# Routing stage of a fused four-layer kernel: three parties of expert places, all shared-expert steps in one stage

## The reference

```
logits = flat @ router_w                       # 2048 x 64 experts
_, topk_idx = top_k(logits + router_bias, 4)   # 4 experts for each token
comb = softmax scores of those 4, made to sum to 1
g = silu(flat @ wg[e]);  u = flat @ wu[e]
routed = sum over e of comb * ((g * u) @ wd[e])
shared = sum over s of (silu(flat @ swg[s]) * (flat @ swu[s])) @ swd[s]
out = routed + shared
```

## Time and profile before

| | us |
|---|---|
| runs shown | 1292.83, 1293.5, 1296.53 (median 1293.5) |
| profiled execution | 1294.35, with a span of 1292.6 |
| busy: TensorE, VectorE, ScalarE, GpSimd | 1117.1, 867.2, 615.2, 407.7 |
| routing stage | 234 to 357.4, the experts' first load at 361.5 |
| stage behind the experts | first gather at 497.3, last at 596.3 |

### The profile page before, as it was taken

One profiled execution on the slowest core, in us unless ns is written; L12 is line 12 of the kernel. 1 busy time (PEld: TensorE's weight loads), 2 busy tenths in 40 slices (PEclk: granted clock), 3 DMA queues, 4 the chain that ended last, 5 costly groups with the idle time before them and its releaser, 6 DMA issues. The chain is left out here.

```text
span 1292.6 us, 31608 instructions
## 1 busy us (share of the span) xinstructions
PE 1117.1 (86%) x12162; PEld 916.7 (71%) x12162; DVE 867.2 (67%) x2172; ACT 615.2 (48%) x1404; POOL 407.7 (32%) x592
## 2 busy tenths in 40 slices
PE   5569998547689997777779999999999999999987
PEld 4446776445478996665547888888888888888776
DVE  5467997757646766688556667666766686664565
ACT  4434455222234443466735554555455555553654
POOL 3331122067700455784038005400530152000221
PEclk9879999757889998888789999999999999999999
DMA  6747785222289884354233334233352342232001
GB/s 161 182 125 203 215 230 185 98 74 90 93 330 417 292 280 164 104 177 143 87 108 110 94 95 143 85 85 105 124 156 85 112 118 91 84 103 84 1 17 50
DMA packets 78562, 177.74 MB, mean 138 GB/s; under 512 B 12678, under 2 KB 26246, under 8 KB 75846
## 3 DMA queue, kind: packets, MB, share of 16 engines
q1 hardware_dynamic: 72140, 158.67, 38.6%
q0 software_dynamic: 6272, 17.05, 4.4%
HBM read 114.40 MB, written 61.08 MB: 136 GB/s over the span
## 5 line engine op out<-in xcount | busy, mean ns | idle before, releaser
L2318 ACT ACTIVATE decay<-masked,negcum 128x128 f32<-128x128 f32 x512 | 163.1, 391 | 102.8 <-DVE mixT L2382 102.8
L2226 PE MATMUL joint<-xh,w_high 128*128 128x512 f32 x512 | 209.3, 409 | 2.0 <-POOL wl L2162 2.0
L2226 PE MATMUL joint<-xl,w_high 128*128 128x512 f32 x512 | 200.2, 391 | 0.0
L2226 PE MATMUL joint<-xh,wl 128*128 128x512 f32 x512 | 199.9, 390 | 0.0
L2430 DVE COPY cT<-joint 128x512 f32<-128x512 f32 x128 | 88.3, 690 | 86.0 <-PE joint L2226 85.7
L2336 ACT ACTIVATE bT<-joint 128x512 f32<-128x512 f32 x128 | 76.6, 599 | 129.9 <-PE joint L2226 129.9
L2382 DVE TENSOR_TENSOR mixT<-pcb,decay 128x512 f32<-128x512 f32 x128 | 82.4, 685 | 57.8 <-PE pcb L2242 57.8
L2159 POOL TENSOR_TENSOR w_high<-w_in,none 128x512 fp32r<-128x512 f32 x32 | 37.0, 1155 | 260.4 <-DMA w_in<-in_w_bc 250.0
L2226 PEld LDWEIGHTS joint<-xh,w_high 128*128 128x128 f32 x512 | 96.2, 188 | 23.6 <-POOL wl L2162 2.4
L2226 PEld LDWEIGHTS joint<-xh,wl 128*128 128x128 f32 x512 | 96.1, 188 | 20.8
L2226 PEld LDWEIGHTS joint<-xl,w_high 128*128 128x128 f32 x512 | 96.3, 188 | 17.0
(11 more groups left out here) (373 smaller groups left out, 2715.7 us busy)
## 6 DMA issues: line engine op xcount, KB each, us to landing
cumrow<-ssm_cum SPq DMA_DIRECT2D x128, 256.0 KB, 3.3
slots_in<-blank SPq DMA_DIRECT2D x16, 1024.0 KB, 5.6
rows<-slots_in SPq DMA_DIRECT2D x32, 512.0 KB, 5.1
slots_out<-spare SPq DMA_DIRECT2D x32, 512.0 KB, 3.8
weights<-in_expert_quads SPq DMA_DIRECT2D x16, 768.0 KB, 9.1
w_in<-in_w_bc SPq DMA_DIRECT2D x32, 256.0 KB, 3.7
qk_parts<-parts SPq DMA_DIRECT2D x32, 192.0 KB, 2.3
stack<-qk_parts SPq DMA_DIRECT2D x32, 192.0 KB, 5.4
```

Of the source, the lines that this page charges most:

```text
L2226: last = nc.tensor.matmul(bank[:], w[:, j, col:col + P], a[:, k, c * CHUNK:(c + 1) * CHUNK], start=(m == 0), stop=(m == len(parts) - 1))
L2318: last = nc.scalar.activation(decay[:, n % 2, o], masked[:, n % 2, o], ACT.Exp, bias=negcum[:, c * TPC + i, head:head + 1])
```

## The change

Expert places are given out in three parties of 1, 1 and 2 chunks (`PARTY`); counts and ranks are summed by party. All 16 shared steps run in the routing stage: steps 0 to 3 (chunk 0) ahead of chunk 2's transposes, the other twelve behind `place_chunk(3)`. On VectorE a step is cut into `product` and `low`, which are spread between other work, one `low` even inside `find_slots`. The deviations of x of chunks 2 and 3 stand ahead of scatters 12 and 16. In the stage behind the experts the splits, the late steps, their loads and their copies are gone, and `first` is (0, 2, 2, 0).

```diff
-PARTIES = 2
+PARTY = [0, 1, 2, 2]
+PARTIES = PARTY[-1] + 1
-BEFORE_ROWS = 6
-LATE = 2
-NOW = NCH - LATE
+BEFORE_ROWS = {12: 2, 16: 3}
...
-    STEPS = SHARED * NOW
+    STEPS = SHARED * NCH
...
-                            if n == BEFORE_ROWS:
-                                for late in range(EARLY_NORMS, NCH):
-                                    deviations(OF_X, late)
+                            if n in BEFORE_ROWS:
+                                deviations(OF_X, BEFORE_ROWS[n])
...
                 turn(0)
                 turn(1)
                 score(0)
-                score(1)
                 place_chunk(0)
+                score(1)
+                pe.wait_ge(logits_out, 1)
+                up(0)
                 place_chunk(1)
-                turn(2)
-                score(2)
-                turn(3)
-                score(3)
+                pe.wait_ge(logits_out, EARLY_NORMS)
+                for n in range(1, SHARED):
+                    up(n)
+                    down(n - 1)
+                down(SHARED - 1)
+                pe.wait_ge(y_out, 1)
+                turn(2)
+                turn(3)
+                score(2)
+                score(3)
                 place_chunk(2)
                 place_chunk(3)
                 pe.wait_ge(logits_out, NCH)
...
+                for n in range(SHARED, STEPS):
+                    up(n)
+                    if n > SHARED:
+                        down(n - 1)
...
+                step(0)
+                step(1)
+                step(2)
+                step(3)
+                fill_rows(2)
+                take(0)
+                fill_rows(3)
+                high_parts(2)
+                high_parts(3)
...
-                    first = (2, 2, 2, 0)[g]
+                    first = (0, 2, 2, 0)[g]
...
-                for n in range(LATE_STEPS):
-                    late_step(n)
-                late_down(LATE_STEPS - 1)
```

More of the change, by code:

```diff
@@ L921, in tiles, with party_of @@
             return slice(g * TPC, (g + 1) * TPC)
+        def party_of(g):
+            chunks = [c for c in range(NCH) if PARTY[c] == PARTY[g]]
+            return PARTY[g], chunks[0] * TPC, (chunks[-1] + 1) * TPC
         def normed(kind, g):
@@ L1001, in rank @@
                         to = j + 1 - n * TB
[L1002 to L1006, removed]
+                        if to < till:
+                            last = nc.tensor.matmul(ps[n][:, to:till, :], sums[:, 1, :],
+                                                    chosen[:, j:j + 1, :].broadcast_to([P, till - to, NE]),
+                                                    start=False, stop=(to == till - 1), skip_group_check=True)
+                    if end == (g + 1) * TPC:
                         last.then_inc(ranks_done, 1)
@@ L1105, in take, with step @@
                     last.then_inc(y_out, 1)
-                for n in range(STEPS):
+                def step(n):
                     act.wait_ge(gate_done, n + 1)
@@ L1115, in _ @@
                     nc.scalar.activation(hh[:, n % 2, :], prod[:, n % 2, :], ACT.Copy).then_inc(hi_done, 1)
-                    if n == 1:
+                high_parts(0)
+                high_parts(1)
+                scale_y(2)
+                scale_y(3)
+                step(0)
[7 more added lines that the diff above has]
+                high_parts(3)
+                for n in range(SHARED, STEPS):
+                    step(n)
+                    if n == 2 * SHARED - 1:
                         act.wait_ge(shifted, 1)
                         nc.scalar.activation(flat(expd[:]), flat(logit[:]), ACT.Exp).then_inc(exp_done, 1)
-                    if n % SHARED == 0 and n:
+                    if n % SHARED == 0 and n > SHARED:
                         take(n // SHARED - 1)
-                take(NOW - 1)
+                take(NCH - 1)
             @block.vector
@@ L1207, in find_slots @@
                     link(last)
+                    between()
                     spots = [spot[:, n, part, :] for n in range(3)]
@@ L1241, in step @@
                                             ALU.subtract).then_inc(lo_done, 1)
+                def step(n):
+                    product(n)
+                    low(n)
                 statistics(y, OF_Y, 2)
@@ L1251, in _ @@
                 add(2)
-                choose(1)
                 tables(0)
                 find_slots(0)
+                choose(1)
+                step(0)
+                tables(1)
+                product(1)
+                find_slots(1, lambda: low(1))
+                product(2)
                 statistics(x, OF_X, 2)
+                low(2)
+                product(3)
                 add(3)
+                low(3)
                 statistics(x, OF_X, 3)
-                find_slots(1)
@@ L1259, in _ @@
                 low_parts(2)
+                low_parts(3)
                 choose(2)
-                low_parts(3)
                 choose(3)
-                tables(1)
-                find_slots(2)
-                step(0)
-                find_slots(3)
-                step(1)
+                tables(2)
+                product(4)
+                find_slots(2, lambda: low(4))
+                product(5)
+                find_slots(3, lambda: low(5))
+                product(6)
                 find_owners()
+                low(6)
@@ L1286, in _ @@
+                for n in range(10 + TOPK, STEPS):
+                    step(n)
                 dve.wait_ge(owner_turned, 1)
@@ L1918, in convolve @@
                             n += 1
-                for s in range(SHARED):
-                    split(s)
                 dve.wait_ge(raw_loaded, 16)
```

198 lines of the change are left out of this document (46 added, 152 removed).

## The result

The kernel after takes 1297.9 us in the median of 20 runs (1294.5 to 1303.1), against 1293.1 for the kernel before (20 runs); the ratio is 1.0044, with a 95% interval of 1.003 to 1.0058. So it is slower by some 5.7 us (the two medians alone differ by 4.8). Forecast were 1300 us and a chance of 0.66 for slower. The profiled execution, with a span of 1301.3 us, is the longest of the 20, so the two profiles differ by more than the medians do.

A forecast was written before the change was run, and what follows sets the result against it. GpSimd was taken as the bound, by scatters in routing and gathers behind the experts. Routing +1.4, experts 0 and the stage behind +5.3 gave +6.7, from the median 1293.5 to 1300 us, range 1293 to 1306.

The forecast's parts named there:

- Routing, +1.4: Routing stage: chunk 2's slots come later than their slack allows, moving the 33rd scatter from 309.50 to 310.9, +1.4 us.
- GpSimd's power and product, 1.4, and up to 1 us for a scatter in the way (280.5): Routing: GpSimd's deviation hop between VectorE's second statistics (278.5) and ScalarE's four rows, ending at 280.5.
- The bounds (-4 and +7): Routing term's limits: -4 us if scores run at TensorE's upper clock, +7 if steps 1 to 3 stay at the lower.
- The late steps, right: Behind the experts: the eight late shared steps lie in the shadow of GpSimd's gathers, which bound that stage.
- Rival 2: Behind the experts: GpSimd isn't the bound and chunk 0's 6 us carry through every chunk, 1289 us; chance 0.10.
- Stage behind, +5.3: Behind the experts: GpSimd idles 7.2 us for chunk 0's statistics, less 0.9 and 1.0 won back, 5.3 us later.
- a gain of 1 us, at most 3: Behind the experts: the first 16 gathers run faster without splits and late steps beside them, 1 us, at most 3.
- Rival 1: Lighter stage and other interleaving speed the later 48 gathers by 3.9 us, 1296.3, no change that can be told; chance 0.24.
- The steps behind chunk 3's slots, right: Routing: ten steps behind chunk 3's slots end near 360 on TensorE, hidden by 3 us before the experts' load.
- rival 3: Routing: shared steps at the old 5.77 us interval end the stage, 11 us behind the rows, 1311 us; chance 0.06.
- Experts: Experts' stage: four loads of 384 KB fewer near its end, taken as 0, at best a gain of 0.3 us.
- The signs: Profile marks of a right forecast: GpSimd's two waits, first scatter near 256, chunk 3's gather wait, experts 1 to 2 us later.

The follow-up runs named there:

- e11: The kernel after run once more, unchanged, for a second profile; 101.8 us from first to last gather, no whole time given.
- e3: The kernel after with one tile gathered ahead of chunk 0's first deviation behind the experts; 1291.8 us, ratio to before 1.0005.
- e10: The kernel before run once more, unchanged, for a second profile; 99.1 us from first to last gather, no whole time given.
- e1: The kernel before with no tiles gathered ahead of chunk 0's first deviation behind the experts; 1302.2 us, ratio to before 1.0084.
- e2: The kernel before without the splits, eight late shared steps and their two copies behind the experts; ratio to before 0.9983.
- e4: The kernel after with chunk 3's deviation of x ahead of scatter 14 instead of 16 in routing; 1295.2 us, ratio to before 1.003.
- e9: The kernel of e7 with the softmax and share work of the routing stage on PSUM; 1285.5 us, ratio to before 0.9953.
- e6: The kernel after with routing reordered: statistics and steps 1 to 3 ahead of the second party's tables, deviations before scatters 5 and 9; 1293.9 us, ratio 1.0019.
- e7: The kernel after with e6's routing order and e3's one tile gathered ahead; 1286.65 us, ratio to before 0.9961.
- e5: The kernel after with two parties of two chunks again, deviations of x ahead of scatters 6 and 10; 1303.6 us, ratio to before 1.0087.
- e12: The kernel of e9 measured once more, unchanged; 1285.1 us, ratio to before 0.9953.
- e8: The kernel after with the low part of steps 8 to 15 reading a PSUM bank instead of the product; 1297.7 us, ratio to before 1.0042.

## Why the prediction was right, and where it was off

**The sum.** By the table, after (with e11, e3) against before (with e10, e1, e2): to the 33rd scatter 78.3 against 74.9, +3.4; the intervals 46.3 against 45.9, +0.4; the experts 142.3 against 142.9, -0.7; gathers 101.75 against 99.0 (unedited ones only), +2.7. Together +5.8, where the ratio gives +5.7. Forecast were +1.4, 0, 0 and +5.3. The total came near because these two terms missed in opposite directions, which is luck. That 5.8 meets 5.7 is luck as well: the stretches outside the table, ahead of the routing stage and behind the last gather, are 1.1 shorter and 1.8 longer in these profiles of after, and vary by 3 to 5 us between all profiles.

**Routing, +1.4 against +3.8.** The mechanism is the one forecast: scatters with idle time for chunk 2's slots, 6.96 us against "some 6". The first scatter came at 256.94 against 256. VectorE's chain up to the second statistics was counted to 278.5 and came to 279.9: 1.0 from chunk 0's choice, in a stage that began at TensorE's lower clock in this execution, 0.4 from the tables. (In e11, which began at the upper one, that choice starts 7.5 us behind the first transpose instead of 9.7, and the 33rd scatter stands at 77.9 instead of 79.8.) The step that was too short is the next one: "GpSimd's power and product, 1.4, and up to 1 us for a scatter in the way (280.5)". The deviation stands behind scatters 14 and 15, each of which waits for a transfer, and it ended at 284.2, 2.3 more than the 1.4 carried over explain. The hop from ScalarE's rows to the score was 2.1 and not 3.7, which took 1.6 back. The scores start at 288.36 against 286.3, and the slots follow 24.9 us later against 24.5. e4 shows it: with two scatters less in the way the deviation ends 2.8 us earlier and the wait for slots is all but gone, with help from the clock. The bounds (-4 and +7) held it.

**TensorE's clock.** The scores ran at the lower level as taken: 5.1 us from one chunk's choice to the next (2.33 of it idle), 0.21 us from one matmul to the next. That the steps before it ran at the upper level (granted 1.00 from 270 to 280) did not carry over: TensorE then waited 3.6 us for chunk 3's rows, up to 285.3, and the granted clock fell in that time (0.64 from 280 to 290). No run tells this wait from other causes of the fall.

**The late steps, right.** e2 and e1 show it from both sides: taking them out brings 2 us, and idle time of GpSimd lengthens the stage. Rival 2 falls with them.

**Stage behind, +5.3 against +2.7.** The idle time (7.08) and its price (e3 gives back 5.2 for 5.3 us of it) are right. The term that was mis-sized is the gathers' gain: "a gain of 1 us, at most 3". All 64 gathers are held by 6.4 us in after and by 10.5 in before, 4 us less; 3.6 of them lie in the 48 later gathers, where I had expected no change (between e10 and e11 it is 3.4, with 1.8 there). By what VectorE was doing at each long gather, two things went. The late steps' splits and low parts held 1.2 us in e10 and 1.7 in before, and are not there in after. VectorE's sums into y, the same in both kernels, held 3.5 and 4.6 and now hold 2.2 to 2.4, since other gathers begin inside them. The two edits of before part them: e1, with all late steps and another interleaving, is held by 7.4 in all and by 1.7 in these sums; e2, with before's order and no late steps, by 7.6 and 3.3. So 7.1 - 0.9 - 4 = 2.2, where 2.7 was measured; the difference is open. Rival 1 had this, with 3.9 us and for both reasons, the lighter stage and the other interleaving; its "against", that the later chunks have the same sums beside their gathers, doesn't hold, since it matters which gathers begin inside them. With the routing's larger loss it didn't win in the total. The Trainium skill (SBUF — State Buffer, SBUF: two separate sides) has the rule that I quoted; the way to size the term by it is to list which VectorE operations have two SBUF inputs, and which gathers begin inside one. I used it for a direction alone and called the sum little.

**The steps behind chunk 3's slots, right.** The interval with the share work is 4.98, against the 5.0 counted; the last low part ends at 360.27 (359.58 + 0.69), and TensorE, done with the last step near 362, stands idle for 4.83 us until the experts' rows let it go on at 366.65, so rival 3 falls.

**Experts.** Four loads less and 0.7 us shorter, where 0 to 0.3 was said. Not tested further.

**The signs.** The wait ahead of the 33rd scatter, the one ahead of chunk 0's first deviation, the first scatter and chunk 3's wait for a gather came as said. Chunk 0's projection starts at 544.7 instead of 545.3, chunk 1's at 580.8 instead of 572.3, as said. The experts' start came 5.2 us later by the clock, where 1 to 2 was said; that is the routing term again.

**The better version.** e9 has all 16 shared steps in the routing stage and three parties, as after, and is 0.5% faster than before. So moving the work need not cost time; of the loss in after, the written order around it is what e3, e4, e6 and e7 give back. Whether the move gains anything by itself isn't shown: no run has the better orders with the late steps where before has them.

## To carry to other kernels

An engine that is never idle for data in a stage can be its bound even when its instructions are tiny. Work of other engines beside it then costs little (e2), and time in which it waits comes back in the stage's length (e3: 5.2 us for 5.3; e1: 8.2 for 10.7, the rest won back by gathers held less). So a small instruction that waits must stand where its input is just ready, neither earlier (e5) nor behind the queue of transfers (e4). When slack of 8 us stands ahead of a consumer and a change uses 10 of it, count every instruction ahead of each hop. Beside indirect transfers of GpSimd, count VectorE's operations with two SBUF inputs, and move one input to PSUM where a bank is free; e9 and e12 show the shorter transfers by this, not a shorter kernel.

## What the runs showed of the hardware

- A scatter (128 rows, indirect) that GpSimd begins while VectorE is in an operation with two SBUF inputs takes the rest of that operation and 0.83 us (130 of 153 in 14 profiles), unless the operation began only some 0.05 us before it or less; otherwise it takes 0.96. An operation with one input in PSUM doesn't hold it: of 128 scatters that begin inside a reduction, a step's product or one of the operations that e8 and e9 moved to PSUM, 121 take up to 0.97 and 6 take 1.03 (the last, the first scatter of e5, takes 1.22). In e9, held is 1.1 instead of 4.1 to 6.8.
- A cast with one SBUF input held a gather as well. VectorE and GpSimd in before:

```profile
501.63 1.36 DVE L1923 CAST wh<-wraw 128x2304 fp32r<-128x2304 f32 x1 [0.69 <-DMA wraw<-in_w_in]
```

```profile
502.06 1.74 POOL L1582 DMA_INDIRECT back<-slots_out,slots  x1 [0.30 <-issue]
```

  Here 0.93 of rest and 0.81 make 1.74. This cast writes 2304 columns in 1.36 us, the subtraction with two inputs behind it takes 2.55. Reductions of 1024 columns, at a slower pace (1.22 us), hold nothing (345.91 in e8). The Trainium skill (SBUF — State Buffer, SBUF: two separate sides) names such casts too, as operations in a 2-port mode; this trace agrees.
- TensorE's clock at the start of routing differs between executions of one kernel. The first eight transposes of the stage in before:

```profile
234.36 1.06 PE L971 MATMUL acc<-ident,rows 128*128 128x128 f32 x8 [1.05 <-PEq L521]
```

  and in its second profile (e10):

```profile
232.31 1.94 PE L971 MATMUL acc<-ident,rows 128*128 128x128 f32 x8 [1.06 <-PEq L521]
```

  That is the upper and the lower level. In this pair it cost nothing, since e10's clock was at the upper level again for the scores: chunk 0's choice starts 8.1 us behind the first transpose in before and 7.5 in e10. Where the scores ran at the lower level too (after, e2, e5, e8, e9) it starts at 9.7, against 7.5 to 8.2 in the other nine profiles. With the wandering start of the stage it is one reason why a term of 1 or 2 us can't be read from a single pair of profiles.
